# Gram matrices of the text tokens: one product of 154 columns and one of 4 in place of three of 77

## The reference, cut to what matters

```python
text_ehs = encoder_hidden_states[:, :-NUM_TOKENS]     # 73 tokens
ip_ehs   = encoder_hidden_states[:, -NUM_TOKENS:]     # 4 tokens
qsem = _l2norm(jnp.einsum('bhst,bte->bhse', probs_t, text_ehs))
sem  = jnp.einsum('bhse,bne->bhsn', qsem, _l2norm(ip_ehs))
```

## Time and profile before

| | us |
|---|---|
| median of 3 runs | 2363.0 |
| all runs | 2359.95, 2363.0, 2370.69 |
| the profiled execution, its own time | 2361.01 |
| its span, first to last instruction | 2359.2 |
| outside the span | 1.8 |
| first instruction of the second stage (on SP and DVE) | about 321.4 |
| PE busy in the whole span | 2195.6 (93%) |
| DVE, ACT, POOL busy | 1847.1, 1722.0, 1595.4 |
| Gram products, 768 of them, busy time by record | 30.2 + 30.0 + 30.0 |

### The profile page before, as it was taken

One profiled execution on the slowest core, in us unless ns is written; L12 is line 12 of the kernel. 1 busy time (PEld: TensorE's weight loads), 2 busy tenths in 40 slices (PEclk: granted clock), 3 DMA queues, 4 the chain that ended last, 5 costly groups with the idle time before them and its releaser, 6 DMA issues.

```text
span 2359.2 us, 86688 instructions
## 1 busy us (share of the span) xinstructions
PE 2195.6 (93%) x32824; PEld 1391.5 (59%) x32824; DVE 1847.1 (78%) x3709; ACT 1722.0 (73%) x2732; POOL 1595.4 (68%) x1056
## 2 busy tenths in 40 slices
PE   7999967999999999999999999999999999999984
PEld 5777744555555555555555555555555555555542
DVE  6856644788888888888888888888888888888874
ACT  4323325888888888888888888888888888888862
POOL 4221224777777777777777777777777777777763
PEclk9999988999999999999999999999999999999997
DMA  8877642444444444444444444444444444444431
GB/s 278 259 235 210 204 128 64 113 119 122 120 120 117 122 124 121 118 124 124 123 122 123 116 122 119 124 124 116 121 123 117 118 124 119 119 124 123 122 88 58
DMA packets 338309, 310.66 MB, mean 132 GB/s; under 512 B 180224, under 2 KB 281856, under 8 KB 337920
## 3 DMA queue, kind: packets, MB, share of 16 engines
q1 hardware_dynamic: 337920, 305.36, 45.6%
HBM read 164.66 MB, written 105.98 MB: 115 GB/s over the span
## 4 chain that ended last, share of the span: by engine, by line
PE 49%; ACT 12%; issue 10%; DMA 5%; DVE 5%; SPq 3%; POOL 2%; DVEq 0%; ACTq 0%; POOLq 0%
PE psum L1014 16%; PE psum L1118 6%; PE psum L1079 6%; ACT ef L1212 6%; PE psum L1130 6%; PE psum L1100 5%; PE psum L1017 3%; PE psum L1083 2%; ACT ust L1220 2%; DMA r_dram<-rd 2%; PE psum L1038 2%; SPq L940 2%; ACT res L1182 2%; DMA ust<-ust 1%; PE psum L1156 1%
## 5 line engine op out<-in xcount | busy, mean ns | idle before, releaser
L1446 POOL TENSOR_TENSOR e<-ef,eh 73x1024 f32<-73x1024 f32 x320 | 682.7, 2134 | 182.6 <-ACT eh L1227 100.1
L1212 ACT ACTIVATE ef<-psum 73x1024 f32<-73x1024 f32 (+1 forms) x640 | 629.7, 1014 | 172.4 <-PE psum L1083 167.6
L1274 DVE TENSOR_REDUCE mneg<-psum 128x8 f16<-128x616 f32 (+3 forms) x512 | 450.0, 931 | 46.2 <-PE psum L1038 41.5
L1302 DVE TENSOR_TENSOR e<-psum,e 73x1024 f32<-73x1024 f32 x320 | 387.0, 1209 | 94.1 <-POOL e L1446 87.1
L1100 PE MATMUL psum<-ef,values 128*32 128x256 f32 x5120 | 359.6, 386 | 9.6 <-issue 6.3
L1118 PE MATMUL psum<-eh,gram 128*73 128x512 f16 x1280 | 339.3, 388 | 9.7 <-ACT eh L1227 2.3
L1408 POOL TENSOR_TENSOR ust<-ust,rb 128x768 f32<-128x768 f32 x128 | 232.4, 1815 | 169.8 <-DMA ust<-ust 169.3
L1227 ACT ACTIVATE eh<-ef 73x1024 f16<-73x1024 f32 x320 | 336.7, 1052 | 7.7 <-POOL e L1446 0.4
L1413 POOL TENSOR_TENSOR al<-ust,ah 128x768 f16<-128x768 f32 x128 | 210.7, 1646 | 82.0 <-ACT ah L1252 82.0
L1220 ACT ACTIVATE ust<-psum 128x512 f32<-128x512 f32 x384 | 229.1, 597 | 40.4 <-PE psum L1100 31.9
L1079 PE MATMUL psum<-q_low,keys 32*73 32x256 f16 (+3 forms) x3072 | 207.2, 266 | 53.5 <-ACT ust L1220 33.7
(11 more groups left out here) (188 smaller groups left out, 4818.5 us busy)
## 6 DMA issues: line engine op xcount, KB each, us to landing
rb<-r_dram SPq DMA_DIRECT2D x128, 384.0 KB, 4.0
keys<-k_dram SPq DMA_DIRECT2D x128, 231.0 KB, 3.3
values<-v_dram SPq DMA_DIRECT2D x128, 192.5 KB
ust<-ust SPq DMA_DIRECT2D x512, 48.0 KB, 2.9
v_dram<-vst SPq DMA_DIRECT2D x64, 320.0 KB
out<-outt SPq DMA_DIRECT2D x64, 320.0 KB, 2.3
k_dram<-kst SPq DMA_DIRECT2D x32, 616.0 KB, 3.9
x<-in_x SPq DMA_DIRECT2D x32, 384.0 KB, 3.6
```

Of the source, the lines that this page charges most:

```text
L1212: act.activation(ef[l][0:m, unit_heads(n), :].rearrange("t h s -> t (h s)"), src, ACT.Exp, scale=SM).then_inc(s_exp[l], 1)
L1274: dve.tensor_reduce(dst, o, AX_X, ALU.max, negate=True).then_inc(s_max[l], 1)
L1302: dve.tensor_tensor(rest, banks(l, f"u{k}", 2)[0:m, :, :], rest, ALU.mult).then_inc(s_wr, 1)
L1446: pool.tensor_tensor(e2[0:m, k, :, :], ef[1][0:m, unit_heads(k), :], eh[0:m, unit_heads(k), :], ALU.subtract).then_inc(s_e2, 1)
```

## The change

The Gram work of a chunk becomes four uses of two batches each in place of two uses of four. `KV_USES` gets two entries more, so KU is 25 and the values are u 15 to 24; the ring stays 8. `ch` and `cl` become the halves of one tile, so that a single product with weights `ch` reads high and low columns together (2x77=154 columns): its first 77 result columns are high by high, its last 77 high by low. The third product, weights `cl` by `ch`, is made for the 4 image columns only. For G twice high by low stands in for the two mixed products. ACT now copies the high-by-high half out of PSUM into `gsum`; DVE adds for C, forms 2 x mixed + high for G in `gsum`, and writes the two f16 parts from there, waiting on its own results twice.

```diff
-           + [("ki", 1, 0, 0)] + [("g", 1, 0, half) for half in (0, 1)]
+           + [("ki", 1, 0, 0)] + [("g", 1, 0, quarter) for quarter in range(4)]
...
-        ch = sb("ch", [P, 2, EC, CT], F16)
-        cl = sb("cl", [P, 2, EC, CT], F16)
+        chl = sb("chl", [P, 2, 2, EC, CT], F16)
+        ch, cl = chl[:, 0, :, :, :], chl[:, 1, :, :, :]
...
+        gsum = sb("gsum", [P, CB, T])
...
-                results_of("g", 1, 1)
+                results_of("g", 1, 3)
...
-                        for j in range(HB):
-                            t0 = half * HT + j * T
-                            mm = three(psum[0:T, r, j * T:(j + 1) * T],
-                                       [(parts[h1][:, slot, k, t0:t0 + T], parts[h2][:, slot, k, t0:t0 + T])
-                                        for k in range(EC) for h1, h2 in ((0, 0), (0, 1), (1, 0))])
+                        n = TXT[1]
+                        for j in range(2):
+                            t0 = (2 * half + j) * T
+                            own, images = slice(t0, t0 + T), slice(t0 + n, t0 + T)
+                            o = psum[0:T, r, 2 * j * T:2 * (j + 1) * T].rearrange("p (z t) -> p z t", z=2)
+                            for k in range(EC):
+                                pe.matmul(o, ch[:, slot, k, own], chl[:, :, slot, k, own], start=(k == 0), stop=False)
+                            for k in range(EC):
+                                mm = pe.matmul(o[:, 1, n:T], cl[:, slot, k, own], ch[:, slot, k, images], start=False,
+                                               stop=(k == EC - 1))
...
+                    if kind == "g":
+                        b.reached(act, s_taken[False], 2 * TAKEN[False], (slot - 1) * TAKEN[False] + taken(u))
+                        b.reached(act, s_filled, 2 * KU, slot * KU + u + 1)
+                        o = psum[0:T, u % KV_RING, 0:4 * T].rearrange("p (b z t) -> p b z t", b=2, z=2)
+                        act.activation(gsum[0:T, 2 * half:2 * half + 2, :], o[:, :, 0, :], ACT.Copy).then_inc(s_gfirst, 1)
+                        continue
...
-                        o = by_batch(psum[0:T, r, 0:HT], T)
-                        batches = slice(half * HB, (half + 1) * HB)
-                        dve.tensor_scalar(gst[0:T, batches, 0, :], o[:, :, 0:n], GS, None, ALU.mult)\
+                        o = psum[0:T, r, 0:4 * T].rearrange("p (b z t) -> p b z t", b=2, z=2)
+                        batches = slice(2 * half, 2 * half + 2)
+                        done = 4 * slot + half + 1
+                        b.reached(dve, s_gfirst, 8, done)
+                        dve.tensor_tensor(cst[0:T, batches, :], o[:, :, 1, n:T], gsum[0:T, batches, n:T], ALU.add)
+                        dve.scalar_tensor_tensor(gsum[0:T, batches, 0:n], o[:, :, 1, 0:n], 2.0, gsum[0:T, batches, 0:n],
+                                                 ALU.mult, ALU.add).then_inc(s_gsum, 1)
+                        b.reached(dve, s_gsum, 8, done)
+                        dve.tensor_scalar(gst[0:T, batches, 0, :], gsum[0:T, batches, 0:n], GS, None, ALU.mult)\
                            .then_inc(s_ghigh, 1)
-                        dve.tensor_copy(cst[0:T, batches, :], o[:, :, n:T])
-                        b.reached(dve, s_ghigh, 4, 2 * slot + half + 1)
-                        ins = dve.scalar_tensor_tensor(gst[0:T, batches, 1, :], o[:, :, 0:n], GS,
+                        b.reached(dve, s_ghigh, 8, done)
+                        ins = dve.scalar_tensor_tensor(gst[0:T, batches, 1, :], gsum[0:T, batches, 0:n], GS,
                                                        gst[0:T, batches, 0, :], ALU.mult, ALU.subtract)
```

More of the change, by code:

```diff
@@ L304, in keys_and_values @@
         s_vstored = [sem(f"values_stored{l}") for l in both]
-        s_ghigh = sem("gram_high")
+        s_gfirst, s_gsum, s_ghigh = sem("gram_firsts"), sem("gram_sums"), sem("gram_high")
         s_ipsq, s_ipf, s_vip, s_chain = sem("ip_squares"), sem("ip_filled"), sem("vip_read"), sem("ip_chain")
```

## The result

The changed kernel takes 2371.8 us (median of 6 runs, 2368.5 to 2374.3) against 2364.7 for the kernel before (now 6 runs). The ratio is 1.0035, with a 95% interval of 1.0021 to 1.0048: **7.1 us slower**, where 6.4 were forecast. The profiled execution has a span of 2370.9 us, 11.7 more than before. The first stage accounts for 8.7 of them (SP's first instruction of the second stage starts at 329.99 instead of 321.31), the second, unchanged, for the other 3.0.

The account below looks back on a forecast made before the run. The prediction took PE to bound the first stage, with stage two following directly. Chunk 0 +3.35, boundaries +5.2 and products -2.2 summed to +6.4 us, median 2369 us, range 2361 to 2378.

Parts of the forecast that it names:

- seven boundaries: Chunk ends: the next first use waits for the last values in bank 0, 0.74 us each, 5.2 us in sum.
- ring in chunk 0: Chunk 0: short Gram uses wait for banks a late DVE releases; 3.15 + 0.2 = 3.35 us lost.
- products, chunks 1 to 7: PE's Gram products: 3.36 us a chunk against 3.67, 0.31 saved a chunk, 2.2 us over chunks 1 to 7.
- clock in chunk 0: PE's clock in chunk 0: taken as more likely to hold, so nothing in the sum.
- DVE, ACT, SP: New DVE and ACT work and SP's later G store: covered by idle time or other waits, nothing charged.
- The schedule of starts: Chunk 0: Gram uses start at 31.84, 33.70, 35.72 and 37.11, first values at 38.87 instead of 35.72.
- The 0.2 us added for u 9: Chunk 0: the third value use waits for DVE to take an earlier use, losing 0.2 us more.
- a rival with a chance of 0.1: Chunk 0: PE's clock falls, two value uses slowed, +3.4 us more, 2372; chance 0.1.
- The rival in which their load is not hidden: Gram stretch: wide products cost 105 ns each as weight loads are not hidden; sum +15, 2378; chance 0.07.
- the one with nearly free narrow products: Gram stretch: narrow products' loads run under the wide ones, below 10 ns each; -2.2 us, 2361; chance 0.07.
- A quarter: DVE's four instructions for one two-batch Gram use: about 1.1 us, 4.5 a chunk, 2.7 more than before.
- A move of more than 3 us: Stage two: should stay 2037.8 us long; moving by more than 3 us would show the prediction wrong.

Follow-up runs that it names:

- e7: Changed kernel, but in chunk 0 PE makes each Gram product twice: 2368.6 us (1 run), kernel before 2358.8 on the same chip.
- e1: Changed kernel with the ring turned so a chunk's first use waits for a use taken long before: 2356.6 us, ratio 1.0008 to the kernel before.
- e6: Changed kernel without the 4-column products: 2362.9 us (1 run), kernel before 2358.8 on the same chip.
- e2: Changed kernel with DVE squaring the image tokens later, in chunk 1: 2361.3 us, ratio 1.0034 to the kernel before.
- e3: Changed kernel with both the turned ring and the late squares: 2353.6 us, ratio 0.9997 to the kernel before.
- e4: Kernel before with DVE squaring the image tokens later, in chunk 1: 2352.5 us, ratio 0.9989 to the kernel before.
- e5: Kernel before with a chunk's last values filling bank 0 instead of bank 6: 2367.2 us, ratio 1.0035 to the kernel before.
- e8: Changed kernel with Gram uses after the layer-0 values, ring turned, projections split later, squares late: 2357.9 us, ratio 0.9977 to the kernel before.
- e9: Same kernel as e4, run again on the chip of e8: 2358.6 us, ratio 0.9986 to the kernel before.
- e10: e8 with SP's stores in result order (layer-0 values, G and C, layer-1 values): 2356.4 us, ratio 0.9972 to the kernel before.

## Why the prediction was right, point by point

**Sign and size.** Forecast +6.4 us, measured +7.1 (interval 5 to 11). The sign and the two large terms were right for the reasons given. That the two numbers lie 0.7 us apart is luck: the first stage grew by 8.7 us in the profiled execution, 2.3 more than the sum. Its terms, beside what was predicted:

| term | predicted | found |
|---|---|---|
| seven boundaries | +5.2 | +5.6 (0.75 at five of them, 0.9 and 0.96 at the first two) |
| ring in chunk 0 | +3.35 | +3.05 (values start 38.91 for 35.72) |
| products, chunks 1 to 7 | -2.2 | -1.8 (0.26 a chunk) |
| clock in chunk 0 | 0 | +1.8 (e7) |
| DVE, ACT, SP | 0 | 0 (5.4 us of idle left, e1) |

They sum to +8.65 of the 8.7.

**Boundaries.** Worked from two rows, right to 0.01 us in chunks 2 to 7. The first boundary costs 0.9 us (e7, whose clock stayed up, takes 17.21 us from first values to chunk 1, ten value uses 16.30), the one before the image tokens 0.96 (ACT waits 12.47 us for their products instead of 11.51).

**Chunk 0.** The schedule of starts was right for three of the four Gram uses and for the values (the fourth came at 37.30 for 37.11). The 0.2 us added for u 9 was too much: the kernel before waits there too, its ten value uses taking 16.44 us (35.72 to 52.16) and not 16.30. The step that failed is what PE's clock does in this stretch, a term put at nothing in the sum. "At half clock a quarter takes 1.68 us" stood under a rival with a chance of 0.1, on the ground that waits of 1.2 us more likely leave the clock alone. It fell, at 35.9 us. The rival's price was nearly right, though: +3.4 for two value uses slowed, 1.8 found, as the clock was back at 42.7, some 0.5 us into the second (at half clock a value use takes about 3.3 us, an estimate: twice 1.63).

**Products.** The narrow ones were put at 38.2 ns, and cost 35 by the timeline and 37.5 by e6. By the timeline the saving is 0.26 and not 0.31 us because the wide products take some 71 to 72 ns where the line through the earlier trace rows has 66.7. The rival in which their load is not hidden (105 ns) is out by far, and so is the one with nearly free narrow products. The two rules of the Trainium skill, "TensorE: Matmul & The Clock Gate", that the prediction weighed would have misled: by the section "LDWEIGHTS (loading the stationary operand)" a load of 77 columns takes 64 ns, where a whole pair took 35 to 38; by the section "Back-to-back issue gap" a sustained pair takes about 81 ns at 128 columns, where 154 columns took 71 to 72.

**DVE.** A quarter takes 0.90 us where 1.1 was estimated; the cover was ample.

**Stage two.** A move of more than 3 us was named as a sign of being wrong; it moved by 3.0, on the edge. The twelve profiled executions show how little that means: the span less the start of stage two, for the same instructions, is 2037.9 before, 2040.9 changed, 2025.4, 2029.5, 2029.9 and 2031.8 for e1 to e4, 2037.1, 2039.0 and 2038.2 for e5 to e7, 2041.4, 2037.8 and 2036.9 for e8 to e10. It goes with the chip more than with the edit (e1 to e4 on one, e5 to e7 on another), and two kernels whose second stage is the same differ by 3.6 us on one chip (e8, e9). Why it scatters so was not tried.

## What to carry to other kernels

When a list of uses that go round a ring of banks gets longer, work out anew who holds the bank that each turn begins with: one use more or less can put the last result of a turn right before its first product, and the producer then waits out a whole hand-over, here 0.75 us a turn, three times what the edit saved. Cutting a use in half also halves the time in which its slot must come free, so look where the consumer is late, here in the first turn. And put stores into the order in which results come, since a queue that stands before one late result holds back the rest.

## What the runs showed of the hardware that I had not expected

- PE's clock fell to 1.2 GHz in the midst of a busy stage, with three waits of about 1 us and 0.9 us of products between them (changed kernel, e1), and stayed there from 35.9 to 42.7 us. With the same waits filled by repeated products (e7) it held, and the kernel was 1.4 us faster in chunk 0 for doing more. In e3, with waits of 0.82, 0.27 and 0.85 us, it held too.
- A DVE instruction on f16 in SBUF (128x1232, sum of two parts of one tile) takes 0.79 us alone and 1.8 to 2.7 us when it runs wholly under POOL's split of the context.
- Products of 4 columns with 77 weight columns cost 35 to 37.5 ns, nearly what those of 77 columns did (38.2), where the line through the earlier trace rows would ask 4.2 for their columns; and 154-column products among them cost 71 to 72 ns rather than 66.7.
